# Running six expert blocks between the routing steps of the last two graphs

## The reference, cut

```
x = x + _L0_gnn_ref(_layernorm(x), adj, ...)   # three graph layers, adj @ (x @ W) + b, relu between them
x = x + _L0_ffn_ref(_layernorm(x), ...)        # 8 experts, top 2 of a softmax
x = x + _L1_gnn_ref(_layernorm(x), adj, ...)   # attention over the graph, 8 heads
x = x + _L1_ffn_ref(_layernorm(x), ...)        # 64 experts, top 2, and a shared one

def _L0_ffn_ref(x, Wr, br, W1, b1, W2, b2):
    logits = xf @ Wr.T + br
    probs = jax.nn.softmax(logits, axis=-1)
    top2_prob, top2_idx = jax.lax.top_k(probs, 2)
    comb = zeros((n, e)).at[arange(n)[:, None], top2_idx].add(top2_prob)
    h = jax.nn.gelu(jnp.einsum('nd,edh->enh', xf, W1) + b1[:, None, :], approximate=False)
    o = jnp.einsum('enh,ehd->end', h, W2) + b2[:, None, :]
    y = jnp.einsum('ne,end->nd', comb, o)
```

## Time and profile before

| what | us |
| --- | --- |
| median of 3 runs (2052.95 to 2055.96) | 2055.65 |
| span of the profiled execution, first to last instruction | 2048.4 |
| median less the span: launch and end, outside the instructions | 7.25 |
| graph phase on PE, until its last layer matmul | 0 to 462.4 |
| from there to the first expert matmul | 462.4 to 519.8 |
| first experts | 519.8 to about 985 |

### The profile page before, as it was taken

One profiled execution on the slowest core, in us unless ns is written; L12 is line 12 of the kernel. 1 busy time (PEld: TensorE's weight loads), 2 busy tenths in 40 slices (PEclk: granted clock), 3 DMA queues, 4 the chain that ended last, 5 costly groups with the idle time before them and its releaser, 6 DMA issues. The chain is left out here.

```text
span 2048.4 us, 37117 instructions
## 1 busy us (share of the span) xinstructions
PE 1873.7 (91%) x12098; PEld 1415.7 (69%) x12098; DVE 1481.4 (72%) x3283; ACT 1229.7 (60%) x1870; POOL 1044.4 (51%) x1229
## 2 busy tenths in 40 slices
PE   7999999992899999999789999998988699999996
PEld 6998889992788888888435445443433488888863
DVE  6777777863566666667589899899988466666659
ACT  4444444430566666666587887887777167776730
POOL 3356665553233333334465676676743357777730
PEclk9999999995899999999899999999999799999998
DMA  8445434313555555556324223222421076555669
GB/s 313 154 180 187 173 141 140 151 44 110 162 179 184 190 183 175 175 184 225 120 78 136 95 73 114 79 76 95 131 73 37 24 238 207 174 169 159 170 226 361
DMA packets 136807, 311.73 MB, mean 152 GB/s; under 512 B 36030, under 2 KB 66976, under 8 KB 132576
## 3 DMA queue, kind: packets, MB, share of 16 engines
q1 hardware_dynamic: 106144, 267.69, 39.3%
q0 software_dynamic: 30528, 42.37, 6.0%
HBM read 202.59 MB, written 147.56 MB: 171 GB/s over the span
## 5 line engine op out<-in xcount | busy, mean ns | idle before, releaser
L2060 DVE TENSOR_TENSOR c_att<-c_p_s,adj 128x1024 f32<-128x1024 f32 x256 | 300.4, 1215 | 56.8 <-PE c_p_s L1601 56.8
L1877 ACT ACTIVATE c_att<-c_att 128x1024 f32<-128x1024 f32 x256 | 268.6, 1056 | 116.6 <-DVE c_att L2060 109.6
L1177 POOL DMA_INDIRECT moe_y<-b_y,b_goal x144 | 162.3, 1127 | 318.5 <-DVE b_y L1236 283.3
L2422 POOL DMA_INDIRECT moe_y<-adj,d_goal x236 | 239.9, 1016 | 104.1 <-issue 61.9
L216 PE MATMUL b_p_y<-b_w2h,b_hh 128*128 128x256 f32 x576 | 168.2, 292 | 8.3 <-DVE b_hl L222 5.9
L653 POOL DMA_INDIRECT moe_in<-a_xn,a_rows x128 | 141.5, 1105 | 57.5 <-issue 28.9
L222 DVE TENSOR_TENSOR b_hl<-b_ht,b_hh 128x512 fp32r<-128x512 f32 (+1 forms) x160 | 101.5, 639 | 85.3 <-ACT b_ht L1391 85.3
L217 PE MATMUL b_p_y<-b_w2l,b_hh 128*128 128x256 f32 x576 | 160.2, 278 | 0.0
L218 PE MATMUL b_p_y<-b_w2h,b_hl 128*128 128x256 f32 x576 | 160.2, 278 | 0.0
L1560 POOL DMA_INDIRECT moe_in<-c_xn,c_rows x128 | 131.2, 1025 | 50.7 <-issue 36.9
L1614 PE MATMUL c_p_o<-c_att,c_xp 128*32 128x512 f32 x1024 | 138.2, 612 | 6.5 <-ACT c_att L1877 4.3
(11 more groups left out here) (290 smaller groups left out, 5637.9 us busy)
## 6 DMA issues: line engine op xcount, KB each, us to landing
b_w<-in_moe_w SPq DMA_DIRECT2D x80, 512.0 KB, 5.2
moe_in<-b_zeros SPq DMA_DIRECT2D x65, 520.0 KB, 10.9
adj<-in_adj SPq DMA_DIRECT2D x32, 1024.0 KB, 5.7
d_xin<-moe_in SPq DMA_DIRECT2D x38, 520.0 KB, 3.7
b_xin<-moe_in SPq DMA_DIRECT2D x32, 520.0 KB, 5.9
c_g<-moe_y SPq DMA_DIRECT2D x32, 512.0 KB, 6.2
moe_y<-c_zeros SPq DMA_DIRECT2D x32, 512.0 KB
d_w<-in_moe_w SPq DMA_DIRECT2D x64, 256.0 KB
```

Of the source, the lines that this page charges most:

```text
L1177: pool.indirect_dma_start(out=m["moe0_y"], out_offset=bass.IndirectOffsetOnAxis(ap=goal[:, h, t:t + 1], axis=0), in_=y[:, h, t, :], in_off ...
L1877: act.activation(part, part, ACT.Tanh).then_inc(att_ready, 1)
L2060: dve.tensor_tensor(att[:, u % 2, 2 * c:2 * c + 2, :], p_s[:, 2 * c:2 * c + 2, :], adj[:, h, u % T, :].unsqueeze(1).broadcast_to([P, 2, N] ...
L2422: pool.indirect_dma_start(out=m["moe1_y"], out_offset=bass.IndirectOffsetOnAxis(ap=goal[0:n, j, t:t + 1], axis=0), in_=y[0:n, j, t, :], in ...
```

## The change

The graph phase and the first experts become one block of instructions, with no barrier between them. `moe0_in` gets its rows as before, but six blocks of 512 rows are chosen early: `ahead_table` picks them from the counts of the first twelve graphs, in the last couple, after `split_mix`; each is filled by tokens of those graphs. PE transposes this small table (`turn_ahead`) after the first `layer_one` of the last couple. The rest, 34 blocks, comes from `block_table` once all counts are there: eight mixed pairs and nine full pairs. The total of tiles is unchanged (144). The six early blocks are full (4 tiles) and run while graphs 14 and 15 are routed, PE's, ACT's, DVE's and POOL's instructions being written out in one order for each engine. PSUM is shared: an early block's up uses three banks of `p_h` in turn, its results one bank of `p_y` and the fourth of `p_h`. Arriving rows lie in the half of `adj` that the last graph has left, so a load of rows reads `adj<-moe_in`. The early blocks are numbered 0 to 5, the first of the table is block 6. The clearing of the rows behind the experts' last tokens moves into SP's step for block 4, ahead of its load of block 6's rows.

```diff
-    pair(0, True)
-    with eng.Fori(1, MIXED - 1) as q:
+    pair(EP, True)
+    with eng.Fori(EP + 1, EP + MIXED - 1) as q:
...
-        adj = sb(whole, "adj", [P, 2, T, N])
+        room = sb(whole, "adj", [P, 2 * T * N + 2 * T * (DW - D)])
+        adj = room[:, 0:2 * T * N].rearrange("p (two t n) -> p two t n", two=2, t=T)
+        arrivals = room[:, T * N:T * N + 2 * T * DW].rearrange("p (two t d) -> p two t d", two=2, t=T)
...
+def ahead_table(dve, m, f):
...
+    dve.tensor_tensor(layers(full[:, FLAG, 0:n]), c0.unsqueeze(1).broadcast_to([NSLOT, SNAP_LAYERS, E0]),
+                      thr.rearrange("p (i two) -> p i two", two=2)[:, 1:SNAP_LAYERS + 1, 0:1]
+                      .broadcast_to([NSLOT, SNAP_LAYERS, E0]), ALU.is_ge)
+    dve.memset(full[:, ONE, :], 1.0).then_inc(step, 1)
+    dve.wait_ge(step, 1)
+    dve.tensor_tensor_scan(full[:, UNTIL, 0:n], full[:, ONE, 0:n], full[:, FLAG, 0:n], 0.0, ALU.mult, ALU.add)\
+       .then_inc(step, 1)
+    dve.wait_ge(step, 2)
+    dve.tensor_scalar(past[:, 0, 0:n], full[:, UNTIL, 0:n], at, None, ALU.is_le)
+    dve.scalar_tensor_tensor(out=taken[:], in0=full[:, UNTIL, 0:n], scalar=float(EARLY), in1=full[:, FLAG, 0:n],
+                             op0=ALU.is_le, op1=ALU.mult).then_inc(step, 1)
+    dve.wait_ge(step, 3)
+    dve.tensor_reduce(CELL, past[:, 0, 0:n], AX, ALU.add)
+    dve.tensor_reduce(LAYER, layers(past[:, 0, 0:n])[:, :, E0 - 1], AX, ALU.add).then_inc(step, 1)
+    dve.wait_ge(step, 4)
+    dve.scalar_tensor_tensor(out=found[:, 1:2], in0=LAYER, scalar=-float(E0), in1=CELL, op0=ALU.mult, op1=ALU.add)
+    dve.tensor_scalar(BASE, LAYER, float(BLK), None, ALU.mult).then_inc(step, 1)
+    dve.wait_ge(step, 5)
+    dve.scalar_tensor_tensor(out=found[:, 0:1], in0=found[:, 1:2], scalar=float(REGION), in1=BASE,
+                             op0=ALU.mult, op1=ALU.add).then_inc(step, 1)
+AHEAD_FOUND = 6
+def turn_ahead(pe, m, f, p_table):
+    pe.wait_ge(f["s_ahead_step"], AHEAD_FOUND)
+    for i in range(2):
+        mm = pe.transpose(p_table[i][:, 0:EARLY], f["found"][0:EARLY, i:i + 1], m["ident"][0:EARLY, 0:EARLY])
+    mm.then_inc(f["s_ahead_step"], 1)
+def keep_ahead(dve, f, p_table):
+    dve.wait_ge(f["s_ahead_step"], AHEAD_FOUND + 1)
+    dve.tensor_copy(f["ahead"][:, 0, :], p_table[0][:, 0:EARLY]).then_inc(f["s_ahead"], 1)
+    dve.tensor_copy(f["ahead"][:, 1, :], p_table[1][:, 0:EARLY]).then_inc(f["s_ahead"], 1)
...
+        def up_bank(q, h, c):
+            return (KH0 * (2 * q + h) + c) % UP_BANKS if is_early(q) else c
+        def results_at(q, c):
+            if not is_early(q):
+                return p_y[:, TB * c:TB * c + TB, :]
+            return p_y[:, TB:T, :] if c == 0 else p_h[:, UP_BANKS, :].rearrange("p (t d) -> p t d", d=D)
...
+            def clear_tails(experts):
+                sp.wait_ge(f["s_table"], 1)
+                own_wait(sp, mark_sp)
+                for e in experts:
+                    row = sp.value_load(f["tails"][0:1, e:e + 1], min_val=0, max_val=SPARE - BLK)
+                    sp.dma_start(m["moe0_in"][bass.ds(row, HALF), :].rearrange("(p t) d -> p (t d)", p=P),
+                                 zeros[:, 0:HALF // P].rearrange("p t d -> p (t d)")).then_inc(f["s_tail"], 16)
+            def all_rows_there():
+                sp.wait_ge(f["s_tail"], 16 * E0)
+                for h in range(2):
+                    sp.wait_ge(scattered[h], 16 * 2 * T * NQ)
+                own_wait(sp, mark_sp)
...
+                    if is_pair(j, EARLY - 2):
+                        clear_tails(range(E0))
+                        sp.wait_ge(f["s_table"], 3)
+                        all_rows_there()
+                    after, still = pair_after(q, mixed)
+                    load_rows(after, h, still)
...
-            sp.wait_ge(f["s_table"], 3)
-            first = expert_of(sp, f, 0)
-            expert_load(sp, f["w1"][:], a["moe0_w1"], first, f["s_w1_in"])
+            sp.wait_ge(f["s_ahead"], 2)
+            own_wait(sp, mark_sp)
+            first = expert_of(sp, f, 0, 0)
+            expert_load(sp, f["w1"][:], a["moe0_w1"], first, w1_in)
             load_bias(sp, a, f, first, 0)
-            expert_load(sp, f["w2"][:], a["moe0_w2"], first, f["s_w2_in"])
-            for e in range(E0):
-                row = sp.value_load(f["tails"][0:1, e:e + 1], min_val=0, max_val=SPARE - BLK)
-                sp.dma_start(m["moe0_in"][bass.ds(row, HALF), :].rearrange("(p t) d -> p (t d)", p=P),
-                             zeros[:, 0:HALF // P].rearrange("p t d -> p (t d)")).then_inc(f["s_tail"], 16)
-            sp.wait_ge(f["s_tail"], 16 * E0)
+            expert_load(sp, f["w2"][:], a["moe0_w2"], first, w2_in)
+            sp.wait_ge(adj_lo, TB * B)
+            for h in range(2):
+                sp.wait_ge(scattered[h], 16 * T * SNAPPED)
+            own_wait(sp, mark_sp)
+            load_rows(0, 0, False)
+            load_rows(0, 1, False)
+            for q in range(EP):
+                for h in range(2):
+                    one(q, h, False)
+            each_pair(sp, one)
...
-            for k in range(2):
-                for h in range(2):
-                    scatter(NQ - 1, h, k)
-            for h in range(2):
-                pool.wait_ge(scattered[h], 16 * 2 * T * NQ)
+            one(0, 0, False)
+            one(0, 1, False)
+            scatter(NQ - 1, 0, 0, 0)
+            scatter(NQ - 1, 0, 1, 1)
+            one(1, 0, False)
+            scatter(NQ - 1, 1, 0, 2)
+            scatter(NQ - 1, 1, 1, 3)
+            one(1, 1, False)
+            one(2, 0, False)
+            one(2, 1, False)
+            each_pair(pool, one)
...
                 layer_one(q, 0)
+                if last:
+                    pe.wait_ge(rows_ready, B - 4)
+                    turn_ahead(pe, m, f, p_ahead)
...
                 support(q, 1, 1, one_hi, one_lo, sup1_done)
+                if last:
+                    pe.wait_ge(f["s_ahead"], 2)
...
                 layer_out(q, 0)
+                if last:
+                    pe.wait_ge(xt2_ready, B - 2)
+                    turn(0, 0, False)
                 layer_out(q, 1)
...
+            def up(q, h, mixed, chunks=range(KH0)):
...
+                    if is_early(q):
+                        if j == 0 and c < UP_BANKS:
+                            pe.wait_ge(x1_ready, TB * (B - 2) + c + 1)
+                        else:
...
             couples(pe, NQ, couple)
+            up(0, 0, False)
+            turn(0, 1, False)
+            down(0, 0, False, range(0, TB))
+            pe.wait_ge(xl_ready, 2)
             route_turn(NQ - 1, 0, False)
+            down(0, 0, False, range(TB, T))
             route_logits(NQ - 1, 0, False)
+            up(0, 1, False, range(0, 2))
             route_turn(NQ - 1, 1, False)
+            up(0, 1, False, range(2, KH0))
             route_logits(NQ - 1, 1, False)
+            pe.wait_ge(xt2_ready, B)
+            turn(1, 0, False)
+            down(0, 1, False, range(0, TB))
+            pe.wait_ge(lg_ready, B)
             route_counts(NQ - 1, 0)
+            down(0, 1, False, range(TB, T))
+            up(1, 0, False)
+            turn(1, 1, False)
+            down(1, 0, False, range(0, TB))
+            pe.wait_ge(rows_ready, B - 1)
             route_counts(NQ - 1, 1)
+            down(1, 0, False, range(TB, T))
+            up(1, 1, False)
+            turn(2, 0, False)
+            down(1, 1, False, range(0, TB))
+            pe.wait_ge(rows_ready, B)
             turn_table(pe, m, f, p_table, f["s_step"])
+            down(1, 1, False, range(TB, T))
+            up(2, 0, False)
+            turn(2, 1, False)
+            down(2, 0, False)
+            up(2, 1, False)
+            turn(EP, 0, True)
+            down(2, 1, False)
+            pe.wait_ge(f["s_table"], 3)
+            each_pair(pe, one)
...
             couples(act, NQ, couple)
+            split_up(0)
+            split_rows(0, 0, False)
+            split_down(0, 0, False)
+            gelus(0, 0, False)
+            split_rows(0, 1, False)
+            split_up(1)
             evac_router(NQ - 1, 0)
+            split_down(0, 1, False)
             exps(NQ - 1, 0)
+            gelus(0, 1, False, range(0, 2))
             evac_router(NQ - 1, 1)
+            gelus(0, 1, False, range(2, KH0))
+            split_rows(1, 0, False)
             exps(NQ - 1, 1)
+            split_up(2)
+            for q in range(1, EP):
+                for h in range(2):
+                    one(q, h, False)
+            each_pair(act, one)
...
                 split_mix(q, 1)
+                if last:
+                    dve.wait_ge(rows_step, ROWS_STEPS * SNAPPED)
+                    ahead_table(dve, m, f)
                 split_layer(q, 0, one_feat, one_lo)
+                if last:
+                    keep_ahead(dve, f, p_ahead)
...
             couples(dve, NQ, couple)
+            split_up(0)
+            split_rows(0, 0, False)
+            keep_goal(0, 0, False)
```

(66 more changed lines are left out.)

774 lines of the change are left out of this document (410 added, 364 removed).

## The result

The changed kernel takes 2023.03 us (median of 4 runs, 2021.35 to 2024.28), the kernel before, run beside it, 2054.30 us (2052.31 to 2055.96). The ratio is 0.9847, 95% interval 0.9836 to 0.9859: 31.3 us less. The forecast was 2022.0 us, 33.6 us less.

What follows compares the result with a forecast made beforehand. PE sets the pace except in a hole from 462.4 to 519.8 us; block 6 starts at 558.4 instead of 596.6, -38.2 us, plus 4.6 us clock, gives -33.6 us and 2022.0 us; range 2017 to 2027, 8 in 10: 2012 to 2033.

Steps and rivals of the forecast that it cites:

- The sum: Six early blocks end at 558.4 us against 596.6 in the old order: -38.2 us, with the clock -33.6 us.
- The early table: In the last couple PE waits 3.8 us for DVE's table, 4.1 us with two transposes; 2.3 us charged for clock.
- the way to block 0: Block 0's transposes add 0.8 us, its row load is covered, and up starts at 467.3 us.
- Blocks 0 to 2: Early blocks beside routing of graphs 14 and 15: 16.2, 15.8 and 13.8 us, each 12.4 us plus delays.
- Rival 2: DVE paces the early blocks; four blocks take 2 us longer each, time 2030 us; chance 0.25.
- Block 3: Big table on DVE between first and second low part makes PE wait 3.7 us; block takes 16.1 us.
- Blocks 4 and 5: Block 4 plain, 12.4 us; in block 5 PE waits 4.4 us for block 6's rows, behind SP's clearings.
- they are covered, with 12 us to spare: POOL's scatters of graphs 14 and 15 end near 536 us, before the clearings do.
- Rival 1: The two new waits keep the clock, or clearings are covered: 4.6 and 4.4 us return, 2013 us; chance 0.18.
- Rival 3: ACT table switches cost twice their 1.28 us load, 5.2 us in blocks 0 to 2, 2027 us; chance 0.07.
- Rival 4: The clock stays at half through the early blocks, 12 us each, six 74 us; 2092 us, slower; chance 0.02.
- Rival 5: Early rows late or blocks run one after another, only moving the hole; within 4 us of before; chance 0.01.

Runs made afterwards that it cites:

- clear_early: Changed kernel with SP issuing the eight clearings right after block 5's rows, ahead of block 5's weights; 2023.62 us, ratio 0.9849 to the kernel before.
- no_switch: Changed kernel with the router's exp for graphs 14 and 15 replaced by a copy; 2020.27 us, ratio 0.9846 to the kernel before.
- pool_order: Changed kernel with graph 15's first scatter ahead of the preceding block's result scatters on POOL; 2023.41 us, ratio 0.9853 to the kernel before.
- both: Changed kernel with the edits of pool_order and clear_early together; 2015.52 us, ratio 0.9828 to the kernel before.
- all4: Changed kernel with pool_order, clear_early, turn_later and the big table made later, behind block 4's low parts; 2011.89 us, ratio 0.9807 to the kernel before.
- five: all4 with the clearings between the halves of block 5's weights and the big table turned after three chunks of block 4's up; 2010.56 us, ratio 0.9797.
- turn_later: Changed kernel with PE turning the early table after the logits and second layer_one; 2014.58 us, ratio 0.9818 to the kernel before.

## Why the prediction was right, point by point

**The sum.** The up of block 6 was forecast at 558.4 + 4.6 = 563.0 in old times. It came at 566.11, in a trace that was 3.04 us late before the change has an effect: 563.07. The pace behind it held: from layer_one to the last row load the gain was 33.1 us for 33.6. That the up of block 6 agrees to 0.1 us is luck. Block 3 took 1.7 us more than forecast, and in this one execution half clock ended sooner behind the early table, which gave 1.2 us back; `clear_early`, whose PE runs the same work with waits of the same length, gained 31.3 us over the same stretch. (The terms named for blocks 1 and 2 add up to 15.7 and 13.7 us, 0.1 less each than the sums in the forecast.)

**The early table, with the way to block 0**: forecast 4.1 us and 2.3 for the clock, 6.4 in all. DVE took 2.0 us rather than 2.4, the wait 3.33. In the changed kernel's trace up began at 471.43 - 3.04 = 468.39, 1.2 us sooner than 467.3 + 2.3. But six other traces have A 1.6 us longer, and there the price is 6.6 us. Right.

**Blocks 0 to 2**: forecast 16.2, 15.8, 13.8; measured 16.35, 15.08, 14.31 (from the up rows). Right within 0.7 us each, 0.06 in sum, and part of that is luck: by no_switch, the 0.3 us for the table loads in block 1 were not there, and those of block 2, which had no price of their own, cost 1.2 us. Rival 2 wanted two more each and falls.

**Block 3**: forecast 16.1 us with a wait of 3.7. The wait was 3.42, yet the block took 17.77. The step that failed is the clock: 3.42 us of idle also lost it (0.50 at 529 to 531), 1.7 us not charged.

**Blocks 4 and 5**: forecast 12.4 and 16.8 + 2.3 = 19.1; measured 12.49 and 18.68, with a wait of 4.22 for 4.4. The size is right, the reason was not. The step "they are covered, with 12 us to spare" failed: in old times the scatters on POOL ended at 548 (550.96 - 3.04), not 536. The forecast counted four groups of 6 us and the results between them. It left out that the second group of each graph waits until the first has landed: 2.33 us for graph 14 and 5.91 for graph 15. The groups themselves took 6.4 to 7.0 us, label included, and the first started at 508.85, 505.8 in old times. These sum up to the 12 us. The clearings' chain, which the forecast did price, erred twice in opposite ways: it began at 538.99 - 3.04 = 535.95, not 532.3, and from its last issue to the rows passed 4.3 us (pool_order), not 6. It is about as long as the scatters', and either chain alone gives a wait near the forecast 4.4 us: 3.00 in pool_order, 4.24 in clear_early. So this wait was right partly by luck.

**Rival 1** (waits keep the clock, or clearings covered) did not occur. Its second half was wrong as a mechanism too: covered clearings alone gave nothing back (clear_early), where it had 4.4 us; with the scatters early as well it is 6 us (`both`). **Rival 3**: excluded by no_switch. The Trainium skill ("ScalarE: Activation LUTs", "What ACT_TABLE_LOAD costs") states a drain of about 1.38 us beside each load. The rows show none: of the five loads, the two that stand directly between two instructions (at 489.50 and 498.14) take 1.31 to 1.33 us from the end of the one ahead to the start of the next. **Rival 4** did not occur: the clock came back within each block. **Rival 5** did not occur either. The Trainium skill ("TensorE: Matmul & The Clock Gate", "Why this matters for your kernels") states that idle gaps between bursts of matmuls cost the clock, and all three waits (3.33, 3.42 and 4.22 us, with a granted clock of 0.50 behind each) bear that out.

**The span.** It fell by 26.0 us only, where the stretch with the change gained 33.1. Three us were lost before 421 us and 4.0 behind the last row load: 1.6 in attention and 2.9 after it, less 0.5 between. Attention took 586.8 to 589.9 us over the eleven traces with the changed order and 588.3 and 587.9 before, so this part is chance. The rest behind it took 462.7 to 469.2, before 462.9 and 463.2; whether a part of that is due to the change stays open. The medians, 31.3 us apart, stand between.

## What to carry to other kernels

A load that waits for several chains has to be priced from the latest of them, and each of them has to be followed instruction by instruction, with the waits inside it, a wait for a landing above all; two that end close together hide each other, and only an experiment that removes both shows the price. Count a new wait of PE like those here (3.3 to 4.2 us) about one and a half times to twice, for the clock behind it, and then look for other PE work that can stand in front of it: here moving two transposes gave 5.0 to 6.6 us. When waits are removed in a row, the chain that none of them shortens is the floor; shorten that one first.

## What the runs showed of the hardware

**The clock.** Waits of PE of 0.95, 1.80 and 1.27 us, in the stretch of the early blocks of all4, left the granted clock at full; in the same stretch of the other kernels 2.23 us (five), 2.94 (turn_later), 3.0 (pool_order) and all longer ones brought it to half. Behind these single waits it stayed there between 3 and 7 us. The same wait of 3.3 us cost 1.7 us of clock in one execution (A 44.10) and 3.3 us in six others (45.7). For `five`, behind its wait of 2.23 us:

```profile
548.00:550.00 2.00, 2.00 (x11) 2.00 (x11) 1.23 (x1) 0.16 (x1) 1.40 (x2) 0.50 0.66 123
```

The length of the wait does not decide alone. In the third couple of all4, a wait of 1.22 us and one of 0.40 us 6 us later were followed by half clock until 144.8, which cost that couple about 2 us; the ten other traces have the 1.2 us too, and kept full clock there:

```profile
141.24 0.72 PE L230 MATMUL b_p_h<-a_sumh,a_wh 128*128 128x512 f32 x1 [0.40 <-DVE a_suml L236]
```

**A couple that nothing had touched.** All eleven traces with the changed order have a wait that neither trace of the kernel before has, in the third couple:

```profile
135.23 1.09 PE L243 MATMUL b_p_tr<-consts,a_xn 128*128 128x128 f32 x8 [1.22 <-DVE a_xn L270]
```

POOL's scale for that graph comes late there, behind twelve scatters, three of which take 1.9 to 2.1 us in place of 1.0; in the kernel before it is two of the twelve. It costs some 1.2 of the 3 us by which the last couple starts late; the remainder differs from trace to trace. Why one more of these issues is slow than before was not settled.
